# Group-norm statistics of eight images gathered in three stretches in place of two, in a fused attention kernel

## The reference

```python
xg = x.reshape(B, H, W, GROUPS, C // GROUPS)      # 16 groups of 8 channels
mean = jnp.mean(xg, axis=(1, 2, 4), keepdims=True)
var = jnp.var(xg, axis=(1, 2, 4), keepdims=True)
xn = (xg - mean) * jax.lax.rsqrt(var + EPS)
h = xn.reshape(B, H, W, C) * gamma + beta
q, k, v = h @ wq + bq, h @ wk + bk, h @ wv + bv   # per image, 256 pixels each
out = h + softmax(q @ k.T * C ** -0.5) @ v
```

## Time and profile before

| | |
|---|---|
| three runs | 146.60, 147.21, 147.42 us, median 147.21 us |
| profiled execution | 146.52 us, of which the span of its instructions is 144.6 us |
| busy share of the span | PE 92%, PE weight loads 72%, DVE 73%, ACT 72%, POOL 40% |
| granted TensorE clock, mean over the span | 0.998 of full speed |
| first transposed images on PE | 4.87 us |
| first normalisation on ACT | 11.30 us |
| first query product on PE | 12.32 us |
| scores of image 0 on PE | 19.10 us |

### The profile page before, as it was taken

How to read it: one execution, slowest core, us unless ns; L and a number is a source line. 1 busy time by engine, 2 the same in 40 slices (tenths; PEclk the granted TensorE clock), 3 DMA queues, 4 the chain that set the end, 5 groups by cost and what they waited for, 6 DMA issues and landing times.

```text
span 144.6 us, 4108 instructions
## 1 busy us (share of the span) xinstructions
PE 132.7 (92%) x1615; PEld 104.5 (72%) x1615; DVE 105.5 (73%) x249; ACT 103.4 (72%) x286; POOL 57.4 (40%) x91
## 2 busy tenths in 40 slices
PE   7677999999999999779698999999998999999991
PEld 4447999977676767555576996858665766899890
DVE  5775888998226979997588657799999997920062
ACT  0435734799883779869985599999899987676530
POOL 8941994000000000000078888105058776499000
PEclk9999999999999999999999999999999999999999
DMA  4950000000000000000000000000000000000036
GB/s 128 328 204 0 0 7 0 0 2 0 0 5 0 5 0 5 0 0 0 0 5 0 7 0 5 0 0 5 0 0 5 0 5 0 5 5 5 5 99 192
DMA packets 5026, 3.69 MB, mean 26 GB/s; under 512 B 400, under 2 KB 4880, under 8 KB 5008
## 3 DMA queue, kind: packets, MB, share of 16 engines
q1 hardware_dynamic: 3376, 1.78, 4.3%
q10 hardware_dynamic: 1632, 1.66, 3.6%
HBM read 2.39 MB, written 1.05 MB: 24 GB/s over the span
## 4 chain that ended last, share of the span: by engine, by line
PE 63%; DVE 26%; DMA 3%; issue 3%; POOL 1%; ACT 1%; ACTq 0%; DVEq 0%
PE bank L678 10%; PE bank L737 8%; PE bank L623 6%; PE bank L717 5%; PE bank L725 5%; DVE negmax L471 4%; PE bank L689 4%; DMA x_all<-in_x_dram 3%; DVE prob L480 3%; PE bank L662 3%; DVE prob L513 3%; PE bank L696 3%; PE bank L754 3%; DVE probT L494 3%; PE bank L609 2%
## 5 line engine op out<-in xcount | busy, mean ns | idle before, releaser
L332 ACT ACTIVATE prob<-bank,negmax 128x256 f32<-128x256 f32 (+1 forms) x48 | 19.4, 414 | 13.1 <-DVE negmax L471 12.8
L273 POOL TENSOR_TENSOR prob<-prob,inv 128x512 f32<-128x512 f32 x16 | 16.3, 1043 | 19.2 <-DVE inv L523 19.2
L285 POOL TENSOR_TENSOR prob<-xT 128x128 f32<-128x128 f32 x8 | 3.4, 419 | 49.5 <-DVE xT L504 49.4
L678 PE MATMUL bank<-probT,v 128*128 128x256 f32 x64 | 17.0, 388 | 1.8 <-issue 1.8
L623 PE MATMUL bank<-packed,xT 128*128 128x128 f32 x96 | 15.6, 287 | 1.0 <-ACT prob L332 1.0
L340 ACT ACTIVATE kdiag<-prob 32x512 f32<-32x512 f32 x24 | 15.0, 627 | 1.5 <-DVE prob L562 1.2
L717 PE MATMUL bank<-kdiag,qT 128*32 128x256 f32 x256 | 15.5, 382 | 0.0
L623 PEld LDWEIGHTS bank<-packed,xT 128*128 128x128 f32 x96 | 13.2, 191 | 2.9 <-issue 2.0
L678 PEld LDWEIGHTS bank<-probT,v 128*128 128x128 f32 x64 | 10.9, 190 | 4.6 <-issue 3.8
L501 DVE SCALAR_TENSOR_TENSOR xT<-bank,packed,xT 128x256 f32<-128x256 f32 x16 | 7.5, 482 | 7.8 <-PE bank L678 6.7
L471 DVE TENSOR_REDUCE negmax<-bank 128x2 f32<-128x512 f32 (+1 forms) x24 | 12.8, 534 | 0.5 <-PE bank L652 0.3
(11 more groups left out here) (92 smaller groups left out, 294.6 us busy)
## 6 DMA issues: line engine op xcount, KB each, us to landing
out_dram<-x_all SPq DMA_DIRECT2D x8, 128.0 KB, 1.9
packed<-in_pack_dram ACTq DMA_DIRECT2D x1, 708.5 KB, 6.9
x_all<-in_x_dram SPq DMA_DIRECT2D x2, 256.0 KB, 4.6
x_all<-in_x_dram ACTq DMA_DIRECT2D x2, 256.0 KB, 5.6
packed<-in_pack_dram SPq DMA_DIRECT2D x1, 198.0 KB, 5.9
packed<-in_pack_dram ACTq DMA_DIRECT2D x1, 192.0 KB, 6.2
packed<-in_pack_dram ACTq DMA_DIRECT2D x1, 160.0 KB, 3.2
packed<-in_pack_dram ACTq DMA_DIRECT2D x1, 48.0 KB, 5.8
```

The source lines that it names most:

```text
L273: nc.gpsimd.tensor_tensor(p, p, inv[g][:, t, :].unsqueeze(2).broadcast_to([128, HEADS, KEYS]), ALU.mult)\
L332: last = nc.scalar.activation(prob[g][:, t, 0:keys], psum("scores", layer, g)[:, keys * t:keys * t + keys], ACT.Exp, bias=negmax[g][:, t, ...
L678: last = mm(ps[:, 0:TOK], vals[:, k, :], probT[g][:, 0, TOK * k:TOK * k + TOK], start=k == 0, stop=k == TILES - 1)
```

## The change

The four images 0 to 3 are no longer one stretch but two: images 0 and 1, then images 2 and 3. Images 4 to 7 stay one stretch. The two-image stretches use the same instructions with half the columns. DVE's and PE's order at the head is written anew, the group means of images 4 to 7 move from ahead of qk 0 to a place ahead of qk 1, and their group variances from ahead of qk 1 to a place ahead of qk 2. The list of tiles has one more group-means tile and one more group-variances tile. The keep-warm counts become 2, 4, 2, 8 (29 products with the first 13, in place of 31).

```diff
+FIRST_OF = (0, 2, HALF)
+COUNT_OF = (2, 2, HALF)
...
-        sequence.insert(sequence.index(("qk", 0, 1)), ("group var", 0, HALF))
+        sequence.insert(sequence.index(("qk", 0, 1)), ("group mean", 0, HALF))
+        sequence.insert(sequence.index(("qk", 0, 2)), ("group var", 0, HALF))
...
         order = [("xT", 0, 0), ("xT", 0, 2)]
-        order += [("xT", 0, 4), ("group mean", 0, 0), ("xT", 0, 6), ("group var", 0, 0)]
-        order += [("group mean", 0, HALF)]
+        order += [("group mean", 0, 0), ("xT", 0, 4), ("group var", 0, 0), ("xT", 0, 6)]
+        order += [("group mean", 0, 2), ("group var", 0, 2)]
...
+        def stretch_of(g):
+
+            return sum(g >= first for first in FIRST_OF)
...
-            for n in range(2):
-
-                wait_drained(pool, "group var", 0, n * HALF)
-                at = slice(n * HALF, (n + 1) * HALF)
-                nc.gpsimd.tensor_tensor(var_gn[:, at], var_gn[:, at], neg_half[:, :], ALU.pow).then_inc(s_rstd, 1)
+            for g, of in zip(FIRST_OF, COUNT_OF):
+
+                wait_drained(pool, "group var", 0, g)
+                at = slice(g, g + of)
+                nc.gpsimd.tensor_tensor(var_gn[:, at], var_gn[:, at], neg_half[:, 0:of], ALU.pow).then_inc(s_rstd, 1)
...
-                act.wait_ge(s_factors, 2 * (g // HALF + 1))
+                act.wait_ge(s_factors, 2 * stretch_of(g))
...
-            for g in range(HALF):
-                moments(g)
+            moments(0)
+            moments(1)
             deviations(0)
+            moments(2)
+            moments(3)
+            variances(0)
             moments(HALF)
-            variances(0)
+            deviations(2)
+            factors(0)
+            variances(2)
             moments(HALF + 1)
             moments(HALF + 2)
-            factors(0)
+            factors(2)
             moments(HALF + 3)
             deviations(HALF)
             variances(HALF)
...
             def group_means(g):
-                pe.wait_ge(s_moments, g + HALF)
-                averages("group mean", g, stats[:, g:g + HALF, :, 1])
+                last = g + COUNT_OF[stretch_of(g) - 1]
+                pe.wait_ge(s_moments, last)
+                averages("group mean", g, stats[:, g:last, :, 1])
...
-            AFTER = (2, 2, 2, 8, 4)
+            AFTER = (2, 4, 2, 8, 4)
             pe.wait_ge(s_warm, 1)
             keep_warm(FIRST)
             pe.wait_ge(s_packed[CONST_F], 16)
             turn_images(0)
             keep_warm(AFTER[0])
             turn_images(2)
+            group_means(0)
             turn_images(4)
             keep_warm(AFTER[1])
-            group_means(0)
+            group_variances(0)
             turn_images(6)
             keep_warm(AFTER[2])
-            group_variances(0)
+            group_means(2)
             keep_warm(AFTER[3])
-            group_means(HALF)
-            keep_warm(AFTER[4])
+            group_variances(2)
             pe.wait_ge(s_packed[W0], 16)
             for step, layer, g in sequence:
                 if step == "qk":
                     project(layer, g)
+                if step == "group mean":
+                    group_means(g)
                 if step == "group var":
                     group_variances(g)
```

More of the change, by code:

```diff
@@ L426, in deviations @@
             def deviations(g):
-                at = slice(g, g + HALF)
-                dve.wait_ge(s_moments, g + HALF)
+                of = COUNT_OF[stretch_of(g) - 1]
+                at = slice(g, g + of)
+                dve.wait_ge(s_moments, g + of)
                 link(nc.vector.tensor_scalar(stats[:, at, :, 2], stats[:, at, :, 2], 2.0 / TOK, GN_EPS, ALU.mult, ALU.add))
                 wait_filled(dve, "group mean", 0, g)
-                link(nc.vector.tensor_reduce(out=means[:, at], in_=psum("group mean", 0, g)[:, 0:2 * HALF].rearrange(
+                link(nc.vector.tensor_reduce(out=means[:, at], in_=psum("group mean", 0, g)[:, 0:2 * of].rearrange(
                     "p (g h) -> p g h", h=2), op=ALU.add, axis=AX.X))
                 link(nc.vector.tensor_tensor(spread[:, at, :], stats[:, at, :, 1],
-                                             means[:, at].unsqueeze(2).broadcast_to([128, HALF, 2]), ALU.subtract))
+                                             means[:, at].unsqueeze(2).broadcast_to([128, of, 2]), ALU.subtract))
                 link(nc.vector.tensor_tensor(spread[:, at, :], spread[:, at, :], spread[:, at, :], ALU.mult))
@@ L440, in variances @@
             def variances(g):
-                at = slice(g, g + HALF)
+                of = COUNT_OF[stretch_of(g) - 1]
+                at = slice(g, g + of)
                 wait_filled(dve, "group var", 0, g)
-                nc.vector.tensor_reduce(out=var_gn[:, at], in_=psum("group var", 0, g)[:, 0:2 * HALF].rearrange("p (g h) -> p g h", h=2),
+                nc.vector.tensor_reduce(out=var_gn[:, at], in_=psum("group var", 0, g)[:, 0:2 * of].rearrange("p (g h) -> p g h", h=2),
                                         op=ALU.add, axis=AX.X).then_inc(*drained_by("group var", 0, g))
@@ L449, in factors @@
             def factors(g):
-                at = slice(g, g + HALF)
-                dve.wait_ge(s_rstd, g // HALF + 1)
+                of = COUNT_OF[stretch_of(g) - 1]
+                at = slice(g, g + of)
+                dve.wait_ge(s_rstd, stretch_of(g))
                 nc.vector.tensor_scalar(scale_gn[:, at], var_gn[:, at], part["gn_gamma"], None, ALU.mult).then_inc(s_factors, 1)
@@ L591, in averages @@
             def averages(kind, g, of):
-                mm(begin(kind, 0, g)[:, 0:2 * HALF], group_avg, of, start=True, stop=True).then_inc(*filled_by(kind, 0, g))
+                mm(begin(kind, 0, g)[:, 0:2 * COUNT_OF[stretch_of(g) - 1]], group_avg, of, start=True, stop=True).then_inc(*filled_by(kind, 0, g))
             def image_ready(layer, g):
@@ L765, in group_means @@
             def group_means(g):
-                pe.wait_ge(s_moments, g + HALF)
-                averages("group mean", g, stats[:, g:g + HALF, :, 1])
+                last = g + COUNT_OF[stretch_of(g) - 1]
+                pe.wait_ge(s_moments, last)
+                averages("group mean", g, stats[:, g:last, :, 1])
             def group_variances(g):
                 wait_drained(pe, "group mean", 0, g)
-                averages("group var", g, spread[:, g:g + HALF, :])
+                averages("group var", g, spread[:, g:g + COUNT_OF[stretch_of(g) - 1], :])
             def keep_warm(times):
```

## The result

The changed kernel takes 149.14 us in the median of six runs, the kernel before beside it 146.98: a ratio of 1.0124, 95% interval 1.0091 to 1.0157. It is slower, as forecast, and inside the range of 147.1 to 149.4, but outside the narrower 147.9 to 148.7 that the forecast gave its own sum. The loss is 1.8 us by the ratio (1.3 to 2.3 by the interval), where 1.1 was forecast. Executions with a mean granted clock under 0.99 are mostly longer whatever the kernel, so every median, heap and count of runs from here on leaves them out, while the ratios leave out only the longest of them. For the changed kernel three runs remain, with a median of 148.82.

A forecast was written before the change was run, and what follows sets the result against it. It took PE, busy 92% of the span, and the unbroken chain of waits to bound the kernel. The fifth query product's 1.1 us delay, carried whole, added to the 147.21 us median gave 148.3 us; own range 147.9 to 148.7, wider 147.1 to 149.4.

The forecast's parts named there:

- the rival in which the delay is taken up: Slack in layer 0's DVE part or a later wait shrinks the loss to 0.0 to 0.5 us; chance 0.15.
- DVE's late start: Rival: DVE reaches its first qk drain 1.8 us late and carries that through whole, 149.0 us; chance 0.08.
- the number of DVE instructions alone: By a rule of the Trainium skill alone, ten more DVE instructions at 0.2 us each would give 149.2 us.
- the banks: Deciding part: with the new tile list, tiles of layer 0's start wait for banks; the fifth query product comes 1.1 us late.
- the wait for image 3: Group means of images 4 to 7 take bank 1, freed by image 3's normalisation, so can't start before 13.6 us.
- of qk 4 for the drain of qk 0: qk 4 takes bank 0, freed by DVE at 18.02 us, so it starts at 18.0 in place of 16.93.
- the first stretch: Images 0 and 1 at the head: group means on PE at 6.58 us, L432 on DVE at 7.08, L437 at 7.69.
- The rival of the clock: PE's two gaps, about 10.5 to 11.7 and 12.7 to 13.6 us, lower the clock: 149.7 us; chance 0.07.
- The power on two columns: POOL's power for images 2 and 3, taken at the 4-column row's 1.04 us, putting their factors at 11.97 us.
- The way from the group means of images 4 to 7 to the fifth query product: From 13.6 us on PE to bank 0 freed at 18.02: 4.42 us.

The follow-up runs named there:

- experiments 2: Changed kernel with two tiles exchanged, so that the group means of images 4 to 7 take a free bank: 148.18 us, ratio 1.0087.
- experiment 7: Changed kernel with the free bank for the group means of images 4 to 7, two of POOL's clearings late, 16 first keep-warm products: 147.09 us.
- 12: Changed kernel with two of POOL's clearings late and 16 first keep-warm products, banks as they are ("after, both" in the table): 147.55 us.
- 10: Changed kernel with two clearings late, 16 first keep-warm products and the banks of sixteen tiles chosen by hand ("banks chosen"): 146.58 us, ratio 0.9974.
- experiment 8: Kernel before with only the group means and variances of images 4 to 7 moved behind qk 0 and qk 1, in free banks: ratio 1.0024.
- experiment 3: Changed kernel with 16 keep-warm products in the first set in place of 13: 148.39 us, ratio 1.0093.
- experiments 4: Kernel before with 16 keep-warm products in the first set in place of 13: 146.50 to 146.69 us, ratio 1.0002.
- 11: Kernel before with two of POOL's clearings late and 16 first keep-warm products: 146.67 us, ratio 1.0000.

## Why the prediction was right, and where its size was not

**The whole delay is carried.** In every profile left by the rule above, the time of the execution is the start of the fifth query product plus nearly the same rest:

| kernel | fifth query product | execution | rest |
|---|---|---|---|
| before | 16.93 | 146.52 | 129.59 |
| before, 16 products | 16.96 | 146.50 | 129.54 |
| before, clearings late | 17.03 | 146.64 | 129.61 |
| before, place changed | 17.41 | 147.01 | 129.60 |
| after | 19.44 | 149.16 | 129.72 |
| after, second profile | 19.19 | 148.85 | 129.66 |
| after, free bank | 18.52 | 148.19 | 129.67 |
| after, 16 products | 18.71 | 148.40 | 129.69 |
| after, clearings late | 17.89 | 147.57 | 129.68 |
| after, both | 18.17 | 147.84 | 129.67 |
| banks chosen | 16.94 | 146.62 | 129.68 |

That rules out the rival in which the delay is taken up. It rules out too that DVE's late start adds to it by itself: DVE was 18.43 - 15.38 = 3.05 us late at its first drain of qk, and only PE's 2.51 reached the end. The forecast's figure by the number of DVE instructions alone, 149.2 us, met the measured time by coincidence: with the same ten instructions the kernel takes 147.57 us without the hold and 146.58 with its banks chosen. Luck is in the range too: it reached past 148.7 us only to take in DVE's late start, which is not what made the time long.

**The steps, forecast against measured** (start times in us; "no hold" is the changed kernel with the clearings late, its head at the upper level from 6.3 us on):

| step | forecast | after | no hold |
|---|---|---|---|
| group means of images 0 and 1 | 6.58 | 7.20 | 6.75 |
| their first use on DVE, L440 | 7.08 | 7.97 | 7.15 |
| second L452 | 10.65 | 12.10 | 10.56 |
| factors of images 2 and 3, L463 | 11.97 | 13.10 | 11.56 |
| group means of images 4 to 7 | 13.6 | 14.84 | 13.30 |
| first drain of qk, L476 | 17.15 | 18.43 | 16.88 |
| fifth query product | 18.0 | 19.44 | 17.89 |

Without the hold the forecast is within some 0.4 us at every step and 0.11 at the last. Its loss of 1.1 us is then 147.57 - 146.52 = 1.05. The mechanism that it put first, the banks, is shown: the wait for image 3 costs 0.46 us (experiments 2, 7 and 12), all the bank waits together 0.97 (10 and 12). The forecast named both waits, for image 3 and of qk 4 for the drain of qk 0, but priced neither apart, nor the move of the group means on PE (0.48 in experiment 8, about half of it the second wait).

**What was mis-sized.** The step that failed is "the first stretch": "L432 at 7.08". It put the first instruction of the deviations at nothing, in the shadow of PE. L430's row, shown above, was in the timeline of before. I read past it. The change moves that instruction a microsecond ahead, from the end of the clearing into it. This is 0.82 us of the missing 1.4. The other term is the level of the head, 0.73 us: I took the head of one profile for that of every execution. The rival of the clock looked for a fall in the new gaps of PE behind 10.5 us, where none came; the keep-warm products behind 10.6 us ran at full pace. The level that mattered was the one before, and the kernel before meets it as well, in nine of 21 runs. Two smaller errors go one each way. The power on two columns took 0.70 to 0.73 us and not 1.04, so DVE's queue and not POOL set the factors, 0.30 us sooner. The way from the group means of images 4 to 7 to the fifth query product was 4.60 and not 4.42, 0.18 later. Together 0.82 + 0.73 - 0.30 + 0.18 = 1.43, and 19.44 - 18.0 is 1.44.

The level is no cost of the change itself, unless the change makes the lower one more frequent. With 16 products in both kernels it drops out: 148.39 - 146.64 = 1.75 us, of which the hold is 0.84.

From experiment 7, without the hold, the lower level and the wait of the group means for image 3, to the changed kernel the fifth query product goes 17.45, 17.89 (this bank), 18.71 (hold), 19.44 (level). From 16.93 to 17.45 it is the place of the group means and variances on PE, qk 1 holding the variances, and qk 4 waiting for the drain of qk 0. The ten DVE instructions start the last moments 0.91 us later than in experiment 8 (12.02 for 11.11), but these wait for PE's place anyway. Only with chosen banks do they bound it, and then they use up what the earlier first stretch wins.

**Open.** Whether the change makes the slow head more frequent isn't known: both its profiles have it, and its times (six runs, 148.74 to 149.17) show no second heap, nor any near the 148.4 us of experiment 3. With the clearings late and still 13 products, seven of eight runs are 147.43 to 147.59 and one 148.74, and the profile has the upper level. The hold and the slow head may hang together, but no run settles it. One run of the changed kernel with 16 products took 147.55 us, 0.8 less than the others. That would fit an L438 that slips between two clearings, but that run left no profile.

## What to carry to other kernels

When a list deals tiles to banks in turn, a tile added ahead moves every later one to another bank. Write the new pairs down and look at who frees each. Splitting a batch to start sooner pays only if the last part doesn't start later, since what follows waits for that. And read durations against the other rows of the same line: a long one at the edge of another engine's work is a wait that no view calls a wait.

## What the runs showed of the hardware

**A DVE instruction that is held by POOL looks long, not late.** L438 (float32, SBUF to SBUF, 4 columns) lasted 1.40, 0.98, 0.87 and 1.48 us in four profiles, and ended at 7.92 to 7.94 in each, just behind POOL's clearing at 7.90 to 7.91. It lasted 0.17 without that clearing. Not every DVE instruction is held: DVE's own clearings (128x2048) took 1.76 us each beside POOL's. The bn_stats ahead of it, which reads PSUM, was not slowed: 0.76 us for two, as in the earlier trace rows. The Trainium skill ("GPSIMD Engine Reference", 1. Specifications) says that POOL's SBUF interfaces are shared with VectorE and contend with instructions in a two-port mode or with two SBUF inputs; the trace fits that for L438, but no view shows the mode that it ran in.

**The head's level can't be read off the granted clock.** The row says 1.00 in both heads of the kernel before, while four transposes hold PE for 0.47 us in one and 0.9 in the other. It shows in the duration of equal instructions only, and is worth 0.8 us of this kernel's time. With three more keep-warm products ahead of the first transposes no run of the kernel before lay in the upper heap, 16 runs in experiments 4 and 11.

**The power on POOL has a fixed part.** 0.70 to 0.73 us on 2 columns and 1.01 to 1.04 on 4: by an estimate from these two widths, some 0.4 us whatever the columns.
